# The expert numbers of six FFN tiles packed into one register word

## The reference, cut to what matters

```
scores = sigmoid(xt @ gate_w.T)                    # 16 experts
_, idx = lax.top_k(scores + gate_b, 4)             # each row takes four of them
w = take(scores, idx); w = 2.5 * w / sum(w)
for e in range(16):  y += comb[:, e] * (silu_and_mul(xt @ w13[e].T) @ w2[e].T)
y = y + silu_and_mul(xt @ w13_s.T) @ w2_s.T        # the shared expert
```

## Time and profile before

| | |
|---|---|
| median of 3 runs | 5576.75 us (5570.6 to 5587.85) |
| profiled execution, its own time | 5575.25 us |
| its span in the profile | 5573.6 us |
| TensorE busy | 3333.8 us, 60% |
| VectorE busy | 4095.9 us, 73% |
| DMA, mean of 16 engines | 106 GB/s |
| granted TensorE clock, mean | 0.811 of full speed |

### The profile page before, as it was taken

How to read it: one execution, slowest core, us unless ns; L and a number is a source line. 1 busy time by engine, 2 the same in 40 slices (tenths; PEclk the granted TensorE clock), 3 DMA queues, 4 the chain that set the end, 5 groups by cost and what they waited for, 6 DMA issues and landing times.

```text
span 5573.6 us, 71121 instructions
## 1 busy us (share of the span) xinstructions
PE 3333.8 (60%) x20252; PEld 2334.8 (42%) x20252; DVE 4095.9 (73%) x10422; ACT 1939.1 (35%) x4713; POOL 1773.5 (32%) x2760
## 2 busy tenths in 40 slices
PE   7312054374534734154277888786788878887775
PEld 3101032253323533044254655553466545654654
DVE  0899988999889998999546656666666566666433
ACT  3111022132212311022135644563466445554332
POOL 1110012512444024500634143225511453235534
PEclk9655576697767976588688999998899998998987
DMA  1210001263213532155352333322133334333887
GB/s 49 113 48 8 0 18 36 95 175 109 73 57 116 168 90 77 59 165 155 121 164 83 97 112 114 117 77 69 67 100 97 114 106 124 113 102 111 253 244 225
DMA packets 424942, 588.12 MB, mean 106 GB/s; under 512 B 57200, under 2 KB 301040, under 8 KB 424432
## 3 DMA queue, kind: packets, MB, share of 16 engines
q1 hardware_dynamic: 375408, 449.30, 26.8%
q0 software_dynamic: 49152, 134.28, 7.2%
HBM read 374.96 MB, written 208.40 MB: 105 GB/s over the span
## 4 chain that ended last, share of the span: by engine, by line
DVE 43%; PE 30%; issue 10%; POOL 9%; ACT 4%; DMA 3%; SPq 1%; DVEq 0%; ACTq 0%; POOLq 0%
PE psum L1055 5%; DVE rec L1119 5%; DVE rec L1121 5%; DVE skb L1124 5%; DVE rec L1132 4%; POOL xbuck L1702 4%; DVE rec L1135 4%; DVE region L1127 3%; DVE psum L1237 3%; PE psum L1063 3%; PE psum L913 3%; PE psum L965 2%; POOL yg L1712 2%; DVE acc L1404 2%; PE psum L857 2%
## 5 line engine op out<-in xcount | busy, mean ns | idle before, releaser
L1712 POOL DMA_INDIRECT yg<-ybuck,words x512 | 535.3, 1045 | 893.7 <-DMA ybuck<-yrow 535.1
L1055 PE MATMUL psum<-xgT,w 128*128 128x128 f32 x5296 | 768.3, 292 | 78.2 <-issue 30.8
L1055 PEld LDWEIGHTS psum<-xgT,w 128*128 128x128 f32 x5296 | 702.8, 205 | 126.9 <-issue 98.7
L1063 PE MATMUL psum<-w_w2T,hid 128*128 x1324 | 457.7, 429 | 357.1 <-DVE hid L1388 223.3
L1237 DVE CUSTOM_DVE_ANT_0 psum<-psum,xo 128x128 f32<-128x128 f32 (+3 forms) x1024 | 474.6, 517 | 163.2 <-PE psum L934 161.9
L1702 POOL DMA_INDIRECT xbuck<-srow,words x512 | 524.5, 1024 | 152.4 <-issue 124.0
L845 PE MATMUL psum<-w_ident,xn 128*128 128x128 f32 x512 | 106.3, 344 | 761.8 <-ACT xn L1421 754.6
L1549 ACT ACTIVATE region<-psum 128x512 f32<-128x512 f32 (+3 forms) x1024 | 402.7, 437 | 341.4 <-PE psum L953 334.7
L1584 ACT ACTIVATE xgT<-psum 128x256 f32<-128x256 f32 x662 | 252.7, 382 | 710.8 <-PE psum L1045 709.5
L1073 DVE SCALAR_TENSOR_TENSOR sil<-sil,psum 128x128 f32<-128x128 f32 (+1 forms) x465 | 137.1, 295 | 486.4 <-ACT sil L1593 453.1
L1683 POOL TENSOR_SCALAR_AFFINE_SELECT region<-region 128x128 f32<-128x128 f32 x1024 | 290.3, 299 | 633.6 <-ACT region L1549 619.8
(11 more groups left out here) (201 smaller groups left out, 7423.5 us busy)
## 6 DMA issues: line engine op xcount, KB each, us to landing
w<-in_w13T SPq DMA_DIRECT2D x662, 256.0 KB, 3.0
xg<-xbuck SPq DMA_DIRECT2D x662, 128.0 KB, 2.6
ybuck<-yrow SPq DMA_DIRECT2D x662, 128.0 KB
xbuck<-x SPq DMA_DIRECT2D x40, 512.0 KB, 5.3
x_scratch<-res SPq DMA_DIRECT2D x64, 256.0 KB, 2.1
acc<-x_scratch SPq DMA_DIRECT2D x128, 128.0 KB, 2.6
xbuck<-srow,words POOLq DMA_INDIRECT x512
yg<-ybuck,words POOLq DMA_INDIRECT x512, 3.1
```

The source lines that it names most:

```text
L1055: o = e.matmul(psum[:, mi, half], w13[I % 3][:, k, half], xgT[I % 2][:, k, :], start=(k == 0), stop=(k == 1), skip_group_check=True)
L1063: o = e.matmul(psum[:, mi, 0:D], hid[hi][:, 0:128], w2T[:, bass.ds(expert.pop(I), 1), :].rearrange("p a b -> p (a b)"), start=True, stop=True)
L1712: e.indirect_dma_start(yg[y % 5], None, ybuck[g % 2][0:TILES_OF[g] * 128, :], bass.IndirectOffsetOnAxis(ap=posu[g % 2][:, J - ROWS0[g], k: ...
```

## The change: six numbers in one word

The expert numbers are below 16, so six of them fit into 24 bits. A constant matrix `pack` (128 x 14, one more DMA in the setup) takes the place of the identity in the product of `r_expert`: the row that comes out has 14 words instead of up to 79 numbers, and word i is the sum of the expert numbers of tiles 6i to 6i+5, each times a power of 16. TensorE and SyncE read a word at every sixth tile of a group, and get a tile's number from it by a shift and a mask in registers. For the first tile of a word the shift falls away.

```diff
+PACK = 6
+WORDS = -(-TILES // PACK)
...
-    eidx = [words[:, 1152 + i * TILES:1152 + (i + 1) * TILES].bitcast(I32) for i in range(2)]
+    eidx = [words[:, 1152 + i * WORDS:1152 + (i + 1) * WORDS].bitcast(I32) for i in range(2)]
+    pack = words[:, 1152 + 2 * WORDS:1152 + 3 * WORDS]
...
-                o = e.matmul(psum[0:1, mi, 0:n], ecol[0:n, :], ident[0:n, 0:n], start=True, stop=True)
+                o = e.matmul(psum[0:1, mi, 0:WORDS], ecol[0:n, :], pack[0:n, :], start=True, stop=True)
...
             elif name == "t_in":
-                if i % 4 == 0:
+                if i % PACK == 0:
                     pe.wait_ge(s["rv"], RV0[g] + 13 + 4 * GROUPS[g])
-                    for k in range(min(4, TILES_OF[g] - i)):
-                        r = regs[i // 4 % 4][k]
-                        e.reg_load(r, eidx[g % 2][0:1, i + k:i + k + 1])
-                        expert[I + k] = e.snap(r, min_val=0, max_val=NE - 1)
+                    r = regs[i // PACK % 4]
+                    e.reg_load(r, eidx[g % 2][0:1, i // PACK:i // PACK + 1])
+                    word = e.snap(r, min_val=0, max_val=16 ** PACK - 1)
+                    for k in range(min(PACK, TILES_OF[g] - i)):
+                        expert[I + k] = (word >> 4 * k) & 15
...
             elif name == "t_weight":
-                r = regs[I % 4]
-                sp.wait_ge(s["rv"], RV0[g] + 13 + 4 * GROUPS[g])
-                e.reg_load(r, eidx[g % 2][0:1, I - TILE0[g]:I - TILE0[g] + 1])
-                x = e.snap(r, min_val=0, max_val=NE - 1)
+                i = I - TILE0[g]
+                if i % PACK == 0:
+                    r = regs[i // PACK % 4]
+                    sp.wait_ge(s["rv"], RV0[g] + 13 + 4 * GROUPS[g])
+                    e.reg_load(r, eidx[g % 2][0:1, i // PACK:i // PACK + 1])
+                    word = e.snap(r, min_val=0, max_val=16 ** PACK - 1)
+                x = (word >> 4 * (i % PACK)) & 15
                 sp.wait_ge(s["f1"], max(I - 2, 0))
...
                 e.dma_start(upper32, T["upper"]).then_inc(s["d_set"], 16)
+                e.dma_start(pack, T["pack"]).then_inc(s["d_set"], 16)
                 e.dma_start(maskf, T["maskb"]).then_inc(s["d_set"], 16)
```

More of the change, by code:

```diff
@@ L781, in build @@
     ecol = counts[:, 6, 0:1]
-    words = sb("words", [128, 1152 + 2 * TILES])
+    words = sb("words", [128, 1152 + 3 * WORDS])
     cq = words[:, 0:256].rearrange("p (j e) -> p j e", e=NE)
@@ L832, in tensor @@
         e = nc.tensor
-        regs = [[e.alloc_register(f"expert{i}_{k}") for k in range(4)] for i in range(4)]
+        regs = [e.alloc_register(f"experts{i}") for i in range(4)]
         expert = {}
@@ L886, in tensor @@
                 pe.wait_ge(s["oc"], oc)
-                pe.wait_ge(s["d_set"], 144)
+                pe.wait_ge(s["d_set"], 160)
                 for k in range(2):
@@ L1321, in vector @@
                 dv.wait_ge(s["rct"], g + 1)
-                dv.wait_ge(s["d_set"], 144)
+                dv.wait_ge(s["d_set"], 160)
                 e.tensor_copy(n16, psum[:, mi, n:n + NE]).then_inc(s["rv"], 1)
@@ L1359, in vector @@
                 g, mi = u
-                nj, n = 4 * GROUPS[g], TILES_OF[g]
+                nj = 4 * GROUPS[g]
                 c = RV0[g] + 12 + nj
@@ L1365, in vector @@
                     dv.wait_ge(s["ysum"], 4 * ROWS0[g - 1])
-                e.tensor_copy(eidx[g % 2][0:1, 0:n], psum[0:1, mi, 0:n]).then_inc(s["rv"], 1)
+                e.tensor_copy(eidx[g % 2][0:1, :], psum[0:1, mi, 0:WORDS]).then_inc(s["rv"], 1)
                 tmp = wide[:, 0:4 * nj].rearrange("p (j k) -> p j k", k=4)
@@ L1607, in gpsimd @@
                 e.tensor_copy(identb[:, :], ident[:, :]).then_inc(s["set"], 1)
-                po.wait_ge(s["d_set"], 144)
+                po.wait_ge(s["d_set"], 160)
                 e.tensor_copy(upper, upper32).then_inc(s["set"], 1)
@@ L1829, in constants @@
     c["tcol"] = np.arange(128, dtype=np.float32)[:, None]
+    tile = np.arange(128)
+    c["pack"] = ((tile[:, None] // PACK == np.arange(WORDS)) * 16.0 ** (tile[:, None] % PACK)).astype(np.float32)
     c["upper"] = np.triu(np.ones((128, 128), np.float32), 1)
```

## The result

The changed kernel takes 5520.57 us (median of 4 runs, 5515.1 to 5526.31). The kernel before, run beside it, takes 5573.68 us (4 runs, 5565.43 to 5587.85). The ratio is 0.9903 with a 95% interval of 0.9889 to 0.9916: 53 us or 0.97% faster, between 47 and 62 us. The forecast was 19 us (about 5557 us), with a range that ended at 5532 us. The sign was right and the size was not: the gain is nearly three times the forecast.

The account below looks back on a forecast made before the run. VectorE was taken to bound the kernel until 2,680 us; afterwards empty stretches on TensorE, the fullest engine, can count. Terms -31 + 7 - 3 + 1 + 0.5 = -25.5 us, a quarter lost: -19 us, about 5557 us, range 5532 to 5582 us.

Parts of the forecast that it names:

- TensorE's readings, -31 us: TensorE from 2,680 us: waits on "issue" total 34.3 us; fewer readings take away all but 3 us, gain 31 us.
- cover (1.07 us): TensorE's work already queued when a block of four readings begins: block of 1.9 us minus mean wait of 0.83 us.
- A quarter of the gain lost behind: Other waits, POOL's masks and VectorE's maxima, stand close behind and absorb a quarter: -25.5 us becomes -19 us.
- Shifts and masks, +7 us: TensorE's two added register operations, 0.2 us a tile, behind the release at 53 waits; two thirds of 10.6 us counted.
- SyncE, -3 + 1 us: SyncE's queue saves 0.25 us a tile, worth 3 us; operations behind the wait for f1 delay weights, costing 1 us.
- Setup, +0.5 us: One DMA more ahead of the first input, a place in the queue of 0.48 us, on the path.
- Before 2,680 us, nothing: 237 TensorE readings go beside a VectorE 94% busy; counted as nothing, at most 3 us gained or lost.
- the 117 readings: Sign in the changed kernel's profile: 117 readings on each sequencer.
- the issue waits under 8 us: Sign from 2,680 us on: L1069's (old L1063) waits on issue fall from 28.9 us to under 8 us.
- the 36 ns: Sign: a register shift or mask (REGISTER_ALU) would show 30 to 50 ns in the profile.
- Empty time in attention falls by 15 to 25 us: Sign: TensorE's busy time stays, and its empty time in attention, 421 of 2,210 us, falls by 15 to 25 us.
- more than counted: Rival, 12%: waits named `hid` hide another 10 us, nothing lost behind, shifts and masks fold away: -42 us, 5534 us.

Follow-up runs that it names:

- e4: Kernel before, meant to read each number twice on TensorE; the build dropped the first load, so it is the kernel before again: 5571.4 us, ratio 1.0002.
- e3: Kernel before, but TensorE reads one number at each tile instead of four at every fourth, nothing packed: 5533.24 us, ratio 0.9928.
- e7: Changed kernel with each tile's shift and mask worked out ahead of the waits, on TensorE and SyncE: 5525.85 us, ratio 0.9915 to the kernel before.
- e1: Kernel before with only TensorE reading packed words, SyncE still one number a tile, both tables made: 5529.76 us, ratio 0.9928.
- e2: Kernel before with only SyncE reading packed words, TensorE still in blocks of four, both tables made: 5566.73 us, ratio 0.9990.
- e8: Changed kernel with six register operations instead of two behind each tile's release on TensorE: 5544.92 us, ratio 0.9946 to the kernel before.

## Why the prediction was wrong

- **TensorE's readings, -31 us: the step that failed.** Its mechanism was right and its cover (1.07 us) near the measured one, its sum was not. I took the rows that name "issue" (34.3 us) for the cost of all blocks, and put what hides in the 43 waits named `hid` into the range alone, at 10 us. Measured, the blocks left 66 to 68 us empty, and the change takes away all of it but 1 us. The term should have been about -67. The text described the borrowed name, and then sized it by one piece, which is itself one of the misnamed ones: a block of four ran from 5,499.1 to 5,500.8 us there and left TensorE empty for 0.87 us, and the 0.23 us are only what was left after `sil` happened to end.
- **"A quarter of the gain lost behind": right as a share.** Against e4 TensorE's empty time from 2,680 us fell by 49 us (692.1 to 643.3) for some 67 us taken out of the blocks, so 28% were lost. In this pair of traces it is not one share by stage: in attention 43 us of empty blocks gave 25 us of time, in the last stage 23 to 26 us gave 23. In e3, e7 and e1 the last stage gave 7, 12 and 12 us for the same blocks, so this isn't settled. With -67 in place of -31 the forecast's own sum is (-67 + 7 - 3 + 1 + 0.5) x 0.75 = -46 us, 5529 us.
- **Shifts and masks, +7 us.** The price was right: 0.2 us a tile forecast, 0.193 measured. The count was high: 53 waits, a part of which were blocks, against 32 releases from 2,680 us on that carry operations. Leaving them out gave 3 us, give or take 12.
- **SyncE, -3 + 1 us**: e2 gave 0 to -12; e1, which lacks SyncE's part, is 14 us behind the changed kernel, give or take 12, from two groups. SyncE's part is probably of use and above the forecast; its size isn't settled. Its saving in the queue was right: from the end of the row DMA's issue to the weight DMA's, from 2,680 us on, a tile without a reading takes 0.34 us where it took 0.62 (medians), 0.28 us less where 0.25 was forecast.
- **Setup, +0.5 us**: right by the start. The first input's DMA starts at 7.45 us, forecast 7.36 (6.88 before):

```profile
7.45 0.43 SPq L1746 DMA_DIRECT2D xnT<-in_x  x1
```

- **Before 2,680 us, nothing**: right, by the table of start times.

Of the signs that the prediction named, the 117 readings, the issue waits under 8 us and the 36 ns came. "Empty time in attention falls by 15 to 25 us" came at its edge (25 us by the start times), and as much again fell in the last stage, which I had not singled out. Over stretches the chain there is this loop of TensorE and ACT:

```profile
5300.46 1.12 PE psum L1061 x8
5301.58 0.43 PE psum L1069 x2
5302.01 0.23 PE psum L1051 x2
5302.24 0.02 issue
5302.27 0.39 ACT xgT L1590
```

In such a stretch a gap on TensorE is paid. It is not all of the stage: from 5,170 us on the loop's three matmul lines and `xgT` are 54% of the chain, and transfers of `yg`, `acc` and `w` another 19%. By the trace of the changed kernel the last stage's 27 blocks of before gave 23 us, 0.85 us a block, and attention's 79 gave 25 us, 0.32 us a block. That the loop is the reason for the higher price was not tested, and e3, e7 and e1 show 7 to 12 us for these 27 blocks.

Of the rivals, "more than counted" (5534 us) was the near one, and by its own reason.

When a block of readings begins, TensorE has 1.0 to 1.5 us of matmuls in hand (medians) and works on through them, and then nothing new reaches it until the block is over. The first half agrees with the Trainium skill, "Advanced Engine Details and Errata", section Sequencer Loop, by which queued instructions are apart from what the sequencer executes; its last point, that others can be read and queued meanwhile, did not keep TensorE fed in the kernels with blocks of four or more, where the empty time grows with the block (0.44, 2.31 and 2.40 us in attention for blocks of 1.66, 3.53 and 3.48 us).

## What to carry to other kernels

Measure what a row of register reads costs around each of them, by its length and by how long the engine still has work, and not by the name that the profile gives to the gap: half of the cost stood here under the names of other engines. Reads that stood one by one between matmuls left TensorE empty for 1 us in all (5 by the widest count), and rows of four for 66 to 68 us, so take the row apart first. Here that alone gave 40 us, as much as packing on the same engine did on the same chip. A gap removed is not time gained one for one: some 67 us of gaps gave 48 us in one pair of traces.

## What the runs showed of the hardware

- A register reading is 0.30 us and its step with the copy some 0.47 us ((3.53 - 1.66) / 4); an ALU operation in a register shows as 36 ns and takes 0.095 us in a row.
- Long gaps came with a lower clock. With each number read twice, TensorE's granted clock from 2,680 us on was 0.86 instead of 0.90, and 85 of the 190 us were busy time.
- The first microseconds differ from run to run by as much as a small change is worth. These are the L857 matmuls between 20 and 48 us in the trace of before and in e4, one program twice (busy us, mean ns | idle):

```profile
L857 PE MATMUL psum<-w_attn,xnT 128*128 128x512 f32 (+1 forms) x25 | 18.5, 889 | 0.0
```

```profile
L857 PE MATMUL psum<-w_attn,xnT 128*128 128x512 f32 (+1 forms) x44 | 17.5, 520 | 0.0
```

  The means are over two shapes; a batch of four 128x512 matmuls takes 3.78 us in the one (at 26.09 us) and 1.98 us in the other (at 26.31 us), nearly twice as long, as at the lower and the higher of the clock's two levels. The granted clock reads 1.00 from 20 to 48 us in both traces, so it doesn't show the difference, and that it is the clock is argued from the durations alone. By 360 us the first is 10.6 us late, and 8.8 us at the end. Over all 18 traces the 416th VectorE instruction starts between 359.7 and 373.8 us, and e7 and e8 on one chip are 12.5 us apart there. A span of one trace against one other is not good to better than that.
- Chips differ by more than the change. The changed kernel between 5,150 and 5,450 us on three chips (5520.57, 5596.44 and 5626.66 us), columns as above:

```profile
5150.00:5450.00 300.00, 223.96 (x1426) 191.08 (x1427) 128.43 (x399) 110.26 (x350) 142.46 (x155) 0.91 0.91 285
```

```profile
5150.00:5450.00 300.00, 219.34 (x1286) 181.65 (x1285) 111.56 (x345) 94.63 (x302) 128.97 (x150) 0.84 0.78 238
```

```profile
5150.00:5450.00 300.00, 218.06 (x1326) 172.12 (x1324) 117.81 (x393) 99.93 (x309) 127.15 (x179) 0.85 0.68 209
```

  The windows hold somewhat different work, as attention ends at 5,153, 5,181 and 5,212 us; over 300 us from there the granted clock is 0.91, 0.81 and 0.82, at 285, 249 and 242 GB/s. So the slower ones show a lower granted clock and fewer bytes a second in this stage. Which is the cause was not tested.
